# Four batches of gated cross-attention and feed-forward: where the score maxima and the softmax sums are computed in batches 1 to 3

## The reference

```python
# x (4,512,512), ctx (4,1024,512); 16 heads of 32; hidden width 1536
q  = _qdq(layernorm(x)) @ _qdq(wq).T + bq
kv = ctx @ wkv.T + bkv;  k, v = split(kv)
attn = softmax(einsum('bnhd,bmhd->bhnm', q, k) * scale)
o  = einsum('bhnm,bmhd->bnhd', attn, v)
x  = x + tanh(g_xattn) * (_qdq(o) @ _qdq(wp).T + bp)
h  = layernorm(x)
fuse = silu((h @ fp8(gate_w)) * gate_scale) * ((h @ fp8(up_w)) * up_scale)
x  = x + tanh(g_ffn) * ((fuse @ fp8(down_w)) * down_scale)
```

## Time and profile before

| what | us |
|---|---|
| median of three runs | 979.81 |
| profiled execution, its own time | 980.68 |
| its span | 978.9 |
| PE busy | 892.2 (91%) |
| DVE busy | 664.0 (68%) |
| ACT busy | 462.7 (47%) |
| POOL busy | 424.2 (43%) |

### The profile page before, as it was taken

The page is one execution under the profiler, slowest core; times in us unless marked ns, Lnnn a source line. Parts: engine busy times, 40 slices in busy tenths (PEclk is TensorE's granted clock), DMA queues, the critical chain, the costliest instruction groups (busy, mean ns, idle before and its releaser), DMA issues.

```text
span 978.9 us, 13590 instructions
## 1 busy us (share of the span) xinstructions
PE 892.2 (91%) x5184; PEld 319.1 (33%) x5192; DVE 664.0 (68%) x1028; ACT 462.7 (47%) x597; POOL 424.2 (43%) x380
## 2 busy tenths in 40 slices
PE   5987898999999899899999999999999999993898
PEld 2421121135444322235344322224444322221443
DVE  6888968757977857477977856478877844266322
ACT  4547777653233077663322067772432156771330
POOL 1145888740057188800057288900013158820130
PEclk9998999999999999999999999999999999997899
DMA  9234244300311212100221212100210111100001
GB/s 331 78 92 125 87 124 128 106 22 1 83 52 37 95 62 55 29 1 1 69 67 33 92 60 53 40 1 1 54 28 1 39 65 50 49 1 0 1 1 44
DMA packets 36866, 55.27 MB, mean 56 GB/s; under 512 B 8704, under 2 KB 14912, under 8 KB 36800
## 3 DMA queue, kind: packets, MB, share of 16 engines
q1 hardware_dynamic: 34880, 48.10, 16.6%
q0 software_dynamic: 1920, 6.29, 2.3%
HBM read 31.21 MB, written 4.19 MB: 36 GB/s over the span
## 4 chain that ended last, share of the span: by engine, by line
PE 65%; DVE 18%; ACT 10%; issue 4%; POOL 2%; DMA 1%; ACTq 0%; POOLq 0%; DVEq 0%
PE ps L1267 33%; PE ps L1397 9%; PE ps L1414 9%; ACT r L799 6%; DVE mx L1007 5%; PE ps L1378 4%; PE ps L1428 4%; PE ps L1597 3%; POOL acc L653 2%; DVE acc L1141 1%; PE ps L1440 1%; PE ps L1251 1%; DVE r L1169 1%; DVE am L892 1%; DVE r L1015 1%
## 5 line engine op out<-in xcount | busy, mean ns | idle before, releaser
L799 ACT ACTIVATE r<-ps 128x1024 f32<-128x1024 f32 x256 | 254.6, 1022 | 166.2 <-PE ps L1397 148.6
L1007 DVE TENSOR_REDUCE mx<-ps 128x2 f32<-128x1024 f32 x144 | 169.5, 1219 | 39.3 <-PE ps L1378 39.2
L1397 PE MATMUL ps<-qst,kst 97*128 97x512 f16 x512 | 144.7, 386 | 28.0 <-ACT r L799 23.0
L653 POOL TENSOR_TENSOR acc<-r,acc 128x512 f32<-128x512 f32 x108 | 140.6, 1337 | 7.9 <-ACT r L799 7.4
L1414 PE MATMUL ps<-r,vv 128*32 128x512 f32 x1024 | 138.1, 611 | 0.1
L672 POOL TENSOR_TENSOR r<-xq,r 128x512 f16<-128x512 f32 x48 | 55.6, 1159 | 132.3 <-ACT r L847 131.8
L1022 DVE TENSOR_REDUCE mx<-ps 128x2 f32<-128x1024 f32 x48 | 58.7, 1224 | 58.9 <-PE ps L1378 58.9
L1267 PE MATMUL ps<-xs,w_gate 128*128 128x512 f16 x384 | 90.7, 379 | 1.5 <-DVE xs L1201 1.5
L1267 PE MATMUL ps<-xs,w_up 128*128 128x512 f16 x384 | 91.1, 380 | 0.0
L854 ACT ACTIVATE qst<-ps,gs_c 128x512 f32<-128x512 f32 x48 | 33.0, 687 | 121.7 <-PE ps L1267 121.7
L1597 PE MATMUL ps<-w_down,r 128*128 128x512 f16 x384 | 87.7, 380 | 0.0
(11 more groups left out here) (150 smaller groups left out, 1275.3 us busy)
## 6 DMA issues: line engine op xcount, KB each, us to landing
kst<-k_reg SPq DMA_DIRECT2D x192, 64.0 KB
qst<-q_reg SPq DMA_DIRECT2D x192, 32.0 KB
xs<-in_x SPq DMA_DIRECT2D x4, 1024.0 KB, 5.8
xres<-in_x SPq DMA_DIRECT2D x4, 1024.0 KB, 5.2
out<-xres SPq DMA_DIRECT2D x16, 256.0 KB, 2.0
cf<-in_ctxT POOLq DMA_DIRECT2D x14, 256.0 KB, 3.4
acc<-in_down_w SPq DMA_DIRECT2D x10, 256.0 KB, 2.6
acc<-in_ctxT POOLq DMA_DIRECT2D x10, 256.0 KB, 3.3
```

Source lines behind the costliest of these rows:

```text
L653: nc.gpsimd.tensor_tensor(acc[:, j, :], prob[:, i % P_SLOTS, :], other, ALU.add).then_inc(p_pool, 1)
L799: nc.scalar.activation(prob[:, s:s + 2, :], ps[:, score_bank(b, j):score_bank(b, j) + 2, :], ACT.Exp, scale=SCALE).then_inc(exp_done, 1)
L1007: nc.vector.tensor_reduce(mx[:, g % 2, t, half, 2 * k:2 * k + 2], ps[:, QUAD + 2 * k:QUAD + 2 * k + 2, :], AX.X, ALU.max).then_inc(m_free, 1)
L1397: mm = nc.tensor.matmul(bank(score_bank(b, j) + k), kst[0:97, g % 2, j + k, t * P:(t + 1) * P], qst[0:97, g % 2, j + k, :], start=True, st ...
```

## The change

Batch 0 is as before, as are all projections. From batch 1 on:

- All four groups' maxima are computed in the dense stage before, by D, relu and R as in batch 0. There are 34 slots: one in each of K2 to K7, one behind three of every four `GU` products, ten inside the down products. A slot holds R of the step before and D of the next. The intermediate `kept` lies in the second half of `kst`, and the row for a group ("TOP") takes a bank of the ring that the dense products use.
- The attention stage has no maxima. Scores go through three pairs of banks, (0,1), (6,7) and (2,3), and probabilities through three units instead of two.
- PE sums only unit 31. In every group the other units' probabilities are added on 128x1024 (two heads): the first two heads by DVE (7 operations a group, 6 in group 3); the last two heads by DVE for tiles 0 and 1 (one operation), by POOL for tiles 2 to 5, and by DVE again for what is left. `totals` comes one unit later.
- The `kst` copies of group 1 are issued behind the last maximum; the context goes through two buffers, not three.

```diff
-O_BANK, DEN_BANK, QUAD, PAIR = 4, 5, 4, 6
+O_BANK, DEN_BANK, PAIR = 4, 5, 6
+SCORES = ((0,), (0, 6, 2))
...
+def slot(n):
+    g, i = divmod(n, PARTS)
+    turned = [("S", g - 1, 0)] if i == 1 and g else []
+    halved = [("K", 0, 0)] if n == 0 else [("K", g + 1, 0)] if i == 1 and g < G - 1 else []
+    before = [("R",) + DIFFS[n - 1][1:]] if n else []
+    return turned + before + halved + DIFFS[n:n + 1] if n else halved + DIFFS[:1]
+DOWN_AT = {"DOWN0": (2, 6, 10), "DOWN1": (2, 6, 10), "DOWN2": (2, 6), "DOWN3": (1, 8)}
+SLOTS = [f"K{n}" for n in range(2, 8)] + [f"GU{k}" for k in range(2 * FT) if k % 4 != 3]
+SLOTS += [name for name in DOWN_AT for _ in DOWN_AT[name]]
...
-P_SLOTS = 8
-ADDED, ADDED_LAST = (0, 2, 4, 6), (0, 1, 2, 3, 4, 5)
+P_RING = (2, 3)
+for _g in range(G):
+    _last = 7 if _g < G - 1 else 6
+    ADDS[_g, 0] = [("DVE", (0, 1))] + [("DVE", (t,)) for t in range(2, _last + 1)]
+    ADDS[_g, 1] = [("DVE", (0, 1))] + [("POOL" if t < 6 else "DVE", (t,)) for t in range(2, _last + 1)]
...
-CHUNK_BUFFERS = (None, 1, 3, 3)
+CHUNK_BUFFERS = (None, 1, 2, 2)
...
 def add_units(b):   # POOL
-                    for j in range(HG):
-                        nc.gpsimd.tensor_tensor(acc[:, j, :], prob[:, i % P_SLOTS, :], other,
-                                                ALU.add).then_inc(p_pool, 1)
+                for n, (u, h, g, k) in enumerate(ADD_ORDER["POOL"]):
+                    pool.wait_ge(exp_done, pair_count(b, u, 2 * h))
+                    by, m = ADD_INDEX[g, h, k - 1]
+                    pool.wait_ge({"POOL": p_pool, "DVE": p_dve}[by], add_count(b, (by, m)))
+                    sums = acc[:, 2 * h:2 * h + 2, :]
+                    nc.gpsimd.tensor_tensor(sums, prob[:, p:p + 2, :], sums, ALU.add).then_inc(p_pool, 1)
...
+            def add_units(b, u):   # DVE
+                    nc.vector.tensor_tensor(sums, other, prob[:, p:p + 2, :], ALU.add).then_inc(p_dve, 1)
...
+                    if b < B - 1 and t == NT - 1:
+                        sp.wait_ge(m_free, FREE_AFTER[b + 1, STREAM[-1]])
+                        stack(kst, (khi, khi, klo), 1)
```

More of the change, by code:

```diff
@@ L775, in projection_weights @@
                     for half in range(2):
-                        nc.scalar.copy(wpT[:, 2 * half:2 * half + 2, :], bank(step_bank(0, ("W", 0, 0)) + half, dt=BF16).rearrange(
+                        nc.scalar.copy(wpT[:, 2 * half:2 * half + 2, :], bank(PAIR + half, dt=BF16).rearrange(
                             "p (c n) -> p c n", c=2)).then_inc(act_setup, 1)
@@ L835, in _, with ahead @@
                     nc.scalar.copy(x2T[:, 0, c, :], bank(d_bank(b, f"X2T{c}"))).then_inc(x2_hi, 1)
+                def ahead(name):
+                    for part in AHEAD.get(name, []) if b < B - 1 else []:
+                        differences(b + 1, part)
                 if b < B - 1:
@@ L855, in _ @@
                                          scale=gs_c[:, i:i + 1]).then_inc(silu_done, 1)
+                    ahead(name)
                     if i >= 1:
                         f_split(i - 1)
+                    ahead(f"GU{2 * i + 1}")
                 f_split(FT - 1)
+                for t in range(NT):
+                    ahead(f"DOWN{t}")
         @block.vector
@@ L1202, in _, with beside @@
                                             ALU.subtract).then_inc(d_free, 1)
+                def beside(name):
+                    for part in AHEAD.get(name, []) if not last else []:
+                        maxima(b + 1, part)
                 if not last:
@@ L1220, in _ @@
                     name = f"GU{2 * i + 1}"
-                    if not last:
-                        maxima(b + 1, AHEAD.get(f"GU{2 * i}", []))
+                    beside(f"GU{2 * i}")
                     dve.wait_ge(d_full, d_full_count(b, name))
@@ L1233, in _ @@
                     name = f"DOWN{t}"
-                    if not last:
-                        maxima(b + 1, AHEAD.get(name, []))
+                    beside(name)
                     dve.wait_ge(d_full, d_full_count(b, name))
@@ L1321, in difference, with bank_free, turn_maxima @@
                 mm.then_inc(diff_full, 1)
+            def bank_free(b, name):
+                before = d_before(b, name)
+                if before is None:
+                    pass
+                elif before[:2] == "GU":
+                    pe.wait_ge(fu_ready, b * FT + int(before[2:]) // 2 + 1)
+                elif before[:3] == "OQT":
+                    pe.wait_ge(oqt_copied, b * CT + int(before[3:]) + 1)
+                elif before in TURNED:
+                    pe.wait_ge(x_copied, copies_count(b + 1, before))
+                else:
+                    pe.wait_ge(d_free, d_free_count(b, before))
+            def turn_maxima(out, g, full):
+                for t in range(NT):
+                    mm = nc.tensor.transpose(out[:, t * P:(t + 1) * P], mx[:, g % 2, t, 0, :], identf[:, :])
+                mm.then_inc(full, 1)
             def maxima(b, s):
@@ L1328, in maxima @@
                 if kind == "D":
-                    difference(s)
+                    difference(b, s)
+                    return
+                if kind == "S" and b > 0:
+                    name = f"TOP{g}"
+                    bank_free(b - 1, name)
+                    pe.wait_ge(m_free, FREE_AFTER[b, ("R", g, PARTS - 1)])
+                    turn_maxima(bank(d_bank(b - 1, name), HG), g, d_full)
                     return
@@ L1498, in _ @@
                     g, t = divmod(u, MT)
-                    beside = list(UNIT_STEPS.get(u, []) if b else UNIT_ENDS0.get(u, []))
                     scores(b, u, 0)
```

377 lines of the change are left out of this document (171 added, 206 removed).

## The result

The changed kernel took 1010.99 us (median of four runs, 1009.52 to 1011.87); the kernel before, run beside it on the same chip, 979.96 us. The ratio is 1.0314, 95% interval [1.0296, 1.0332]: slower by 3.1%. The forecast was 1017 us.

A forecast was written before the change was run, and what follows sets the result against it. PE was taken to bound the first two stages and nearly fill attention. Profiled 980.7 us plus 19.9 (attention) plus 17.7 (dense stage) gave 1018.3; with the median 0.9 lower, 1017 us. Forecast's range 995 to 1040; 8 in 10, 930 to 1040.

The forecast's parts named there:

- What decides: Attention: whether DVE's and POOL's additions run side by side (under PE's 67.7 us) or one behind the other (83.3 us); taken as mutual holding, 0.60.
- The walk: Attention, additions followed one by one through a group, DVE and POOL in turn: 22.5 us a group where PE needs 16.5.
- Behind group 3: End of attention: 1.8 us for totals and the sums of unit 31, plus 2.5 for POOL's bias additions getting ahead.
- the bias term: End of attention, batches 1 and 2: POOL's L610 issued while DVE still has two additions; 2.5 us, between 0 and 5.0.
- Batch 3: Attention with no x to prepare: 94.4 us, +3.1.
- Dense stage: K2 to K7, feed-forward and down products: +5.9 us a stage, +17.7 in three (bounds 6 and 27).
- The first D's wait: Dense stage, K2: D waits for K1's copy, k_low and the halved difference while PE has half of K2; +1.0 us.
- the waits in the feed-forward: Feed-forward: R ends late on DVE, behind the product of gate and up, when PE wants its bank; +1.5 us (0 to 4).
- No mutual holding: Rival: the adders hardly hold each other up, PE bounds attention at 67.7 us; 926 us in all, chance 0.20 (915 to 940).
- in part: Rival: the adders hold each other up only partly, attention about 84 us a stage; 975 us, chance 0.14 (950 to 995).
- POOL keeping DVE out over several operations: Rival, attention: DVE's exponentials stuck behind, 3 us more a group, 12 a stage; 1053 us, worse than 1040 has chance 0.06.
- The dense stage alone: Rival: only the dense stage loses (+6), attention at its lower bound (-3); 983 us, counted among the partial cases (0.14).

## Why the prediction was right, step by step

- **What decides** was put right: DVE's two-input additions and POOL's hold each other up, in both directions. Additions beside POOL take 2.8 to 3.4 us and at the group's end 2.34/2 = 1.17, as foreseen; the runs in which POOL reads constants and in which it only writes show the cause, which the earlier trace rows had shown only with POOL as the loser. Group 3 of batch 1 is the cleanest place:

```profile
420.71 16.63 DVE L1061 TENSOR_TENSOR acc<-acc,r 128x1024 f32<-128x1024 f32 x6
...
420.98 13.08 POOL L671 TENSOR_TENSOR acc<-r,acc 128x1024 f32<-128x1024 f32 x4 [11.99 <-ACT r L815]
```

  Taken one by one, DVE's first ends at 421.93, POOL's first at 424.16, DVE's second at 425.25, POOL's second at 427.46. Each ends a fixed time behind the other engine's: POOL's 2.2 us, DVE's 1.1. So the one that comes later waits for the whole of the other, as in the rule that the prediction quoted from the Trainium skill ("SBUF — State Buffer", section "Who interferes with whom"); the trace agrees.
- **The group.** The walk gave 22.5 us, 67.5 for groups 0 to 2, and 5.3 for x: 72.8. Measured from DVE's first addition of each group: 23.3, 24.0 and 23.5, that is 70.9. In batch 3, with no x to prepare, they are 22.3, 22.0 and 22.3, that is 66.7 against 67.5; so x costs about 4.2. Three of its twelve scalar operations were held (2.6 us each), the others took 0.41 to 0.54. Group 3: 19.1 forecast, 19.1 measured. Ahead of them 3.5, forecast and measured. The single prices were less right than the sum, and that it came so close is in part luck. A turn of the two engines is 3.3 us and not 3.64, because POOL's part of it is 2.2 and not 2.5: 1.3 us too much a group. Against that, from DVE's last addition to the next group's first are 1.9 to 2.2 us in batch 3, where the walk had 1.1, as totals runs at a lower clock; and group 3 holds 1.1 us of a bias addition that the walk had put behind it.
- **Behind group 3** the forecast had 1.8 for totals and the last sums and 2.5 for the bias additions getting ahead: 4.3. Measured from the start of totals to the stage's end: 3.3, and in that no bias addition at all. Only one of the four held DVE's last addition, for about 1.1 us and inside group 3; the 3.3 are totals and sums at a granted clock of 0.54 (437.5 to 440.7), where 1.8 was their price at the full clock. So the bias term was 1.4 us too large and the clock, which the forecast left out, costs 1.5. Groups 0 to 2 with x (-1.9), this end (-1.0) and 0.2 by which the earlier trace rows cut the stage of before too short make +5.25 of the +8.4.
- **Batch 3**: +3.1 forecast, +1.6 measured: 0.8 less in groups 0 to 2 and 0.9 less behind group 3, against 91.1 before and not 91.3.
- **Dense stage**: 5.9 forecast, 5.07 measured. The first D's wait was 1.0 and came out at 0.92. The changed kernel's chain of waits in the dense stage, down to the slot with the first transpose:

```profile
250.25 0.92 issue
251.17 0.39 PE ps L1350 x2
251.56 2.70 PE ps L1294 x12
254.26 0.32 PE ps L1415 x2
254.58 0.01 PE ps L1350 x2
254.59 2.70 PE ps L1294 x12
...
278.08 0.45 PE ps L1370 x4
```

  R and D side by side cost 0.33 us and about 0.11 at the next product's start, as a Q step did: 251.56 to 254.59 is 3.03, as in the earlier trace rows. Six more slots in the feed-forward make 2.6 us, two transposes there 1.0. The term that failed is the waits in the feed-forward: I took 1.5, and PE waited for DVE for 0.16 us there; R was rarely late. Down products: -1.1 and two more slots, -0.2 in all, against +0.17.
- **Not in the forecast**: 3.4 us in the tail, where no instruction was changed. The granted clock is 0.84 there against 0.91 in the kernel before. In attention PE was idle for 18.9 us instead of 5.4 and its clock 0.88 against 1.00. That the waiting ahead of the tail brings the lower clock about is not shown. From its first transpose to the end the tail takes 99.0 to 99.5 us in the kernel before and in seven of the experiments, and 102.4 to 102.7 in the three kernels where PE waits most in batch 3 (the changed one, POOL with half its share, POOL reading constants; attention at 0.88, 0.95 and 0.81). But it takes 101.3 us in two versions whose attention ran at the full clock throughout (two tiles on PE with the bias additions held, and two score pairs), and 101.0 in the one with memory sets. What sets the tail's clock stays open.
- **The rivals.** "No mutual holding" (926 us) and "in part" (975) are out by the time and by the turns above. POOL keeping DVE out over several operations (1053) is out: they take turns, also where POOL's four bias additions follow one another with no semaphore between them (360.11 to 368.11 above, one DVE addition after each). The copy of the earlier trace rows, which has one input, was kept out over more than one; why the two differ was not tried. The dense stage alone (983) is out: the maxima part is neutral.

The sum was 6.5 us above the profiled execution (1018.3 and 1011.8): 7.5 too much in attention (19.9 forecast, 12.4 measured), 2.5 in the dense stages (17.7, 15.2), less the 3.4 of the tail.

## What to carry to other kernels

Before additions are given to an idle POOL, count what both it and DVE read from SBUF: here each addition on POOL kept DVE from its own for 2.2 us, and DVE would have done it in 1.1. By these numbers 16 of them cost 16 x 1.1 = 18 us a stage (an estimate); the version with all on DVE and the bias additions held is shorter in attention by 16.9, 17.3 and 21.4 us. Give the surplus to PE instead, one tile in eight here, and see that what POOL still has to do falls where DVE is not adding. This contention showed in no wait, only in an operation that is longer than the same one elsewhere; so compare the same line at two places.

## What the runs showed of the hardware that was not expected

- A POOL memory set of 128x512 (0.53 us) leaves a two-input DVE addition at 1.22 us; a POOL addition of the same size takes it to a mean of 1.89 and takes 2.02 itself, instead of the 1.27 of L636 alone.
- Four POOL additions of 128x512 back to back (L636) made six DVE additions 4.3 us longer and took 8.00 us themselves, 4.96 without company. The engines took turns all the same, 2.2 us a turn.
- Where PE had waited, its granted clock fell from the upper of its levels (2.4 GHz) to the lower (1.2): ahead of totals in batch 1 PE was idle for 4.55 us, the granted clock was 0.50 at the end of that (435.0 to 437.4), and 0.54 in the totals and sums behind it; 0.88 is the mean of attention. These totals, eight products that take 0.86 us at the full clock, in the chain of waits of the changed kernel:

```profile
435.06 2.29 DVE acc L1061
437.35 0.14 issue
437.49 1.94 PE ps L1477 x8
```
